# First chunk of a selective-scan layer: channel input projected without its convolution taps, convolution done on the projection by ScalarE and the Vector engine

## What is computed

```python
u, res = jnp.split(x @ W_in, 2, axis=-1)                 # 256 -> 2 x 512 channels
up = jnp.pad(u, ((0, 0), (2, 0), (0, 0)))
u = up[:, :L] * W_conv[:, 0] + up[:, 1:L + 1] * W_conv[:, 1] + up[:, 2:L + 2] * W_conv[:, 2]
u = jax.nn.silu(u)
x_dbl = u @ W_x
dt, Bm, Cm = jnp.split(x_dbl, [DT_RANK, DT_RANK + D_STATE], axis=-1)
delta = jax.nn.softplus(dt @ W_dt + b_dt)
# deltaA = exp(delta * A), deltaB_u = delta * u * B; scan h = deltaA * h + deltaB_u; y = h . C
# y = (y + u * D_param) * silu(res);  y @ W_out;  x + that, layer norm, experts
```

## Time and profile before

| what | us |
|---|---|
| median of 3 runs | 2549.71 |
| lowest and highest run | 2549.22 and 2555.29 |
| span of the profiled execution | 2526.0 |
| first scan of chunk 0 starts, from the span's start | 51.59 |
| PE, DVE, ACT, POOL busy, share of the span | 91%, 87%, 68%, 72% |
| mean granted TensorE clock | 0.970 |

### The profile page before, as it was taken

The page is one execution under the profiler, slowest core; times in us unless marked ns, Lnnn a source line. Parts: engine busy times, 40 slices in busy tenths (PEclk is TensorE's granted clock), DMA queues, the critical chain, the costliest instruction groups (busy, mean ns, idle before and its releaser), DMA issues. The chain is left out here.

```text
span 2526.0 us, 40011 instructions
## 1 busy us (share of the span) xinstructions
PE 2299.8 (91%) x14043; PEld 1789.0 (71%) x14043; DVE 2208.6 (87%) x2980; ACT 1726.0 (68%) x2861; POOL 1808.3 (72%) x859
## 2 busy tenths in 40 slices
PE   8999999999999999999999998643999999999995
PEld 3566666766766766666667666532989989989995
DVE  3899999999999999999999999987687677777775
ACT  3788888888888898888888888733344344334345
POOL 1698998988988989889899899724155445435566
PEclk9999999999999999999999999975999999999998
DMA  2211222222222221122122121112032322322353
GB/s 91 68 54 65 76 67 76 59 68 68 76 68 68 67 76 60 67 78 75 60 76 76 59 68 59 59 67 71 22 72 37 84 67 36 87 65 37 87 172 149
DMA packets 88227, 179.10 MB, mean 71 GB/s; under 512 B 8896, under 2 KB 51136, under 8 KB 88016
## 3 DMA queue, kind: packets, MB, share of 16 engines
q1 hardware_dynamic: 73136, 154.11, 18.5%
q0 software_dynamic: 14880, 22.29, 4.7%
HBM read 140.19 MB, written 36.18 MB: 70 GB/s over the span
## 5 line engine op out<-in xcount | busy, mean ns | idle before, releaser
L444 POOL TENSOR_TENSOR dbu<-du,b_all 128x2048 f32<-128x2048 f32 x255 | 1157.6, 4548 | 154.3 <-DVE hst L710 104.9
L533 ACT ACTIVATE da<-delta,a_neg 128x512 f32<-128x512 f32 x1008 | 689.5, 689 | 158.7 <-DVE hst L710 149.1
L710 DVE TENSOR_TENSOR_SCAN hst<-da,carry,dbu 128x512 f32<-128x512 f32 x504 | 618.0, 1266 | 0.7
L710 DVE TENSOR_TENSOR_SCAN hst<-da,dbu 128x512 f32<-128x512 f32 x504 | 589.0, 1206 | 18.2 <-ACT da L533 14.9
L1944 PE MATMUL gu<-x_part,w_part 128*128 128x384 f32 (+1 forms) x2304 | 492.0, 363 | 5.8 <-POOL w_part L1481 4.1
L1944 PEld LDWEIGHTS gu<-x_part,w_part 128*128 128x128 f32 x2304 | 407.7, 191 | 37.9 <-issue 4.4
L847 PEld LDWEIGHTS hd<-ident,hst 128*128 128x128 f32 x2048 | 236.0, 142 | 249.5 <-issue 118.9
L640 DVE SCALAR_TENSOR_TENSOR yacc<-hd,c_tok,yacc 128x512 f32<-128x512 f32 x512 | 371.8, 726 | 20.0 <-PE hd L847 19.4
L847 PE MATMUL hd<-ident,hst 128*128 128x128 f32 x2048 | 319.4, 279 | 75.5 <-DVE yacc L640 75.2
L789 PE MATMUL gen<-xT,w_u 128*128 128x512 f32 x720 | 359.7, 599 | 3.9 <-issue 2.7
L520 ACT ACTIVATE hTC<-w,c_tok 128x512 f32<-128x512 f32 x512 | 345.2, 674 | 20.6 <-PE w L847 20.6
(11 more groups left out here) (277 smaller groups left out, 2813.5 us busy)
## 6 DMA issues: line engine op xcount, KB each, us to landing
b_all<-b_rows SPq DMA_DIRECT2D x128, 512.0 KB, 3.8
xT<-in_xT SPq DMA_DIRECT2D x16, 514.0 KB, 5.2
xT_r<-in_xT SPq DMA_DIRECT2D x16, 512.0 KB, 5.1
x_rows<-in_x SPq DMA_DIRECT2D x16, 512.0 KB, 4.8
x_dram<-x SPq DMA_DIRECT2D x16, 512.0 KB, 3.0
acc_dram<-x SPq DMA_DIRECT2D x16, 512.0 KB, 4.5
w_raw<-in_wg SPq DMA_DIRECT2D x8, 1024.0 KB, 5.1
w_raw<-in_wu SPq DMA_DIRECT2D x8, 1024.0 KB, 8.0
```

The source lines that it names most:

```text
L444: nc.gpsimd.tensor_tensor(dbu[DBU[n]][:], du[parity][:], b_n, ALU.mult).then_inc(dbu_ready, 1)
L533: nc.scalar.activation(da_bank[t % 2][:], delta[parity][:, t, :], ACT.Exp, scale=a_neg[:, t, n:n + 1]).then_inc(da_ready, 1)
L710: nc.vector.tensor_tensor_scan(hst[DBU[n]][:, t, :], decay[:], dbu[DBU[n]][:, t, :], initial, ALU.mult, ALU.add).then_inc(scanned, 1)
```

## The change

For chunk 0 alone TensorE multiplies the input with the plain `W_in` (8 matmuls in place of 24), as it lies in `w_staging`, and only the input position of the last tap. ScalarE then copies each bank to `u_raw` with the last tap as a scale for each partition, and the Vector engine adds the two other taps with one `scalar_tensor_tensor` each, from the same bank shifted by one and two columns. Silu then reads `u_raw`. The copy of tile t + 1 stands before the Silu of tile t in ScalarE's order. The taps come in a further small weight tile `w_conv` (128 partitions by 12 values), with a DMA of its own. The load of `xT` moves ahead of the broadcast of the taps. `w_u` is made as before, for the chunks after; TensorE waits for it at the end of its lead.

```diff
+        w_conv = sb("w_conv", [P, DT, N_TAPS])
...
             sp.dma_start(w_staging, w_in_d[:, :, 0:DI]).then_inc(w_loaded, 16)
+            sp.dma_start(xT[:], xT_d[:, :, 0:CL + 2]).then_inc(xt_loaded, 16)
+            sp.dma_start(w_conv[:], a["W_conv"]).then_inc(conv_loaded, 16)
             sp.dma_start(gate[:, 0:N_TAPS, :], a["W_convT"].rearrange("(o t) d -> o t d", o=1).to_broadcast(
                 [P, N_TAPS, DI])).then_inc(spread_loaded, 16)
-            sp.dma_start(xT[:], xT_d[:, :, 0:CL + 2]).then_inc(xt_loaded, 16)
...
         def _(act):
-            for t in range(DT):
-                act.wait_ge(ring_full, LEAD.index(f"e{t}") + 1)
-                nc.scalar.activation(u[:, t, :], lead_bank[f"e{t}"][:], ACT.Silu).then_inc(lead_u if t < DT - 1 else u_ready, 1)
+            act.wait_ge(conv_loaded, 16)
+            for t in range(DT + 1):
+                if t < DT:
+                    act.wait_ge(ring_full, LEAD.index(f"e{t}") + 1)
+                    nc.scalar.activation(u_raw[:, t, :], lead_bank[f"e{t}"][:], ACT.Copy,
+                                         scale=w_conv[:, t, N_TAPS - 1:N_TAPS]).then_inc(lead_scaled, 1)
+                if t > 0:
+                    act.wait_ge(lead_conv, t)
+                    nc.scalar.activation(u[:, t - 1, :], u_raw[:, t - 1, :], ACT.Silu
+                                         ).then_inc(lead_u if t < DT else u_ready, 1)
...
+            dve.wait_ge(conv_loaded, 16)
+            for t in range(DT):
+                dve.wait_ge(lead_scaled, t + 1)
+                for back in range(1, N_TAPS):
+                    if back > 1:
+                        dve.wait_ge(lead_tap, t + 1)
+                    nc.vector.scalar_tensor_tensor(
+                        out=u_raw[:, t, back:], in0=lead_bank[f"e{t}"][:, 0:CL - back],
+                        scalar=w_conv[:, t, N_TAPS - 1 - back:N_TAPS - back], in1=u_raw[:, t, back:],
+                        op0=ALU.mult, op1=ALU.add).then_inc(lead_tap if back == 1 else lead_conv, 1)
...
         def _(pe):
             pe.wait_ge(xt_loaded, 16)
-            for tap in range(N_TAPS):
-                pe.wait_ge(taps_ready, tap + 1)
-                for t in range(DT):
-                    for k in range(KD):
-                        last = nc.tensor.matmul(lead_bank[f"e{t}"][:], w_u[:, tap, k, t * P:(t + 1) * P],
-                                                xT[:, k, tap:tap + CL], start=tap == 0 and k == 0,
-                                                stop=tap == N_TAPS - 1 and k == KD - 1)
-                    if tap == N_TAPS - 1:
-                        last.then_inc(ring_full, 1)
+            pe.wait_ge(w_loaded, 16)
+            for t in range(DT):
+                for k in range(KD):
+                    last = nc.tensor.matmul(lead_bank[f"e{t}"][:], w_staging[:, k, t * P:(t + 1) * P],
+                                            xT[:, k, N_TAPS - 1:N_TAPS - 1 + CL], start=k == 0, stop=k == KD - 1)
+                last.then_inc(ring_full, 1)
...
             pe.wait_ge(late_in, N_LATE * 16)
+            pe.wait_ge(taps_ready, N_TAPS)
```

More of the change, by code:

```diff
@@ L232, in attention @@
         spread_loaded = sem("spread_loaded")
+        conv_loaded = sem("conv_loaded")
+        lead_scaled = sem("lead_scaled")
+        lead_tap = sem("lead_tap")
+        lead_conv = sem("lead_conv")
         weights_in = sem("weights_in")
@@ L2033 @@
         "x": g["x"], "xT": padded.reshape(BATCH * (SEQ + 2), DM).T, "W_in": g["W_in"],
-        "W_convT": g["W_conv"].T, "W_x": g["W_x"],
+        "W_conv": g["W_conv"].reshape(DT, P, N_TAPS).transpose(1, 0, 2), "W_convT": g["W_conv"].T, "W_x": g["W_x"],
         "W_dt": g["W_dt"], "b_dt": g["b_dt"].reshape(DT, P).T, "D_param": g["D_param"].reshape(DT, P).T,
```

## The result

The changed kernel took 2538.81 us (median of 4 runs, 2537.26 to 2540.93) against 2551.53 for the kernel before (4 runs, 2549.22 to 2555.29): 12.7 us less. The ratio of the two medians is 0.995; the estimate from all runs is 0.994, with a 95% interval of 0.9929 to 0.9952, which is 12 to 18 us. Timed again in a later series, it took 2510.56 against 2524.74: 14.2 us less, ratio 0.9945 (0.9932 to 0.9959). The forecast was 2537.7 (2533 to 2543).

What follows compares the result with a forecast made beforehand. The Vector engine, 97% busy, was taken to bound the chunk stages, behind a lead of one chain to the first scan at 51.59 us. Saving 12.0 there gave 2549.7 - 12.0 = 2537.7 us, range 2533 to 2543.

Steps and rivals of the forecast that it cites:

- the 23.7 us added to the span: Whole kernel: the run median stood 23.7 us above the profile's span, so this was added to the forecast span of 2514.0.
- What carries over: After the lead: whatever is saved before the first scan shifts all that follows by as much; 12.0 us forecast.
- a sign of being wrong: After the lead: the first scan comes earlier but the distance from there to the end, forecast 2474.4 us, grows.
- Step 1: Loads in the lead: xT, moved ahead, lands at 7.3 us; the taps' broadcast at 9.6, plus 0.1 for w_conv.
- Step 2: TensorE's projection in the lead: 9.7 us from 7.35 in place of 23.4, with the last tile's bank full at 17.05.
- Step 3: Vector engine in the lead: free at 14.0, then eight added instructions of 0.75 us each, 6.0 in all, to 20.0.
- Step 4: ScalarE in the lead: copies and Silus keep ahead of the Vector engine; a possible second table load costs 0.1 us.
- e0: TensorE's projection in the lead: the PSUM bank of tile 0, first to fill and be copied; forecast full at 11.0 us.
- Step 5: End of xd in the lead: only two records remain after the last Silu; xdT copied at 21.8, not 36.65, saving 14.85.
- Step 6: TensorE's clock in the lead: pauses make it fall around xd's end, so 12.0 us is saved, not 14.85.
- rival (a): TensorE's clock in the lead: stays up through the d matmuls, so 14.85 us saved, 2534.9; chance 0.27.
- Rivals (b) to (d): Respectively: no change within 0.3%, 0.08; slower as w_conv shifts SBUF tiles, 2557, 0.03; tiles ready no earlier, 2549.7, 0.02.

Runs made afterwards that it cites:

- series 4: Kernels timed together on a chip numbered 4: four further variants of the changed kernel; the kernel before took 2558.50 us there.
- series 2: Kernels timed together on a chip numbered 8: both kernels again unedited, and two load-order variants; changed 2510.56 us against 2524.74, ratio 0.9945.

## Why the prediction was right

The time and its sign were right, and so was the mechanism: the lead is one chain, it gets shorter, and all that follows moves with it. The forecast for the first scan was 39.6; it came at 37.22, so 14.4 us saved and not 12.0. That the time came out within 1.1 us of the forecast is in part luck. By the medians 12.7 us were saved, by the trace 14.4, and the interval of the ratio covers both. And the 23.7 us added to the span were mostly the long rest of the timed runs; they came out because the runs of the changed kernel in that series had the long rest as well. Step by step:

- **What carries over.** Predicted 1:1. From the first scan to the experts' second load it is 1690.2 to 1692.9 us in all 14 profiles, for first scans between 34 and 53. Shown, within 2.7 us. The distance to the end, which the prediction put at 2474.4, was 2498.3 in the first profile and 2471.9 in the second. The first of these is what the prediction had named as a sign of being wrong; it was the profile that showed it and not the change, since kernels that don't differ there show the same in series 4 and not in series 2. What makes it stays open.
- **Step 1.** xT landed at 7.55 (predicted 7.3), the broadcast at 10.16 (9.7). Both late by 0.3 to 0.5. That w_conv costs 0.1 was right for its place; in another it cost 1.7 to 2.4, by one profile.
- **Step 2.** The projection took 10.1 us (9.7), e3 was full at 17.65 (17.05).
- **Step 3.** The Vector engine began its row at 14.35 (14.0), ended it at 20.46 (20.0); 0.74 to 0.75 each, as taken from L640 in the earlier trace rows.
- **Step 4.** The second table load ran where it was foreseen, 14.96 to 16.24, and cost little: Silu 0 waited for it, copy 2 came late, and the vector row stood still for 0.17 us. The 2.66 us for a switch of the Trainium skill ("ScalarE: Activation LUTs", "What ACT_TABLE_LOAD costs") didn't appear: the next activation started 1.29 us after the start of the load. What I had not foreseen is a load that waits. The first one stood behind the wait for e0 and ran at 11.41, where that of L452 had run at 1.95; it stayed hidden, since the Vector engine wasn't free before 14.35. Why the one waits and the other doesn't is not shown.
- **Step 5.** xdT at 22.28 (21.8): the sum of the small delays above.
- **Step 6, the step that failed.** "I take 12.0: a fall around xd's end." The clock stayed up to 27.2, and rival (a), with 0.27, described what happened: 14.85 by its sum, 14.4 measured. I had reasoned that xd with gaps is thin work, and had read the Trainium skill's warning of idle gaps as one of gaps like these, though it describes longer ones; the gaps were to be 0.65 us and were 0.25 and 0.38. The doubled vector work, with pauses of 1.6 to 1.7 us, shows that the mechanism exists. Its price ahead of the exponential was 2.7 us (2.8 by the prediction), and 0.9 for the last part of xd (0.95). The sum lacks a further 0.9 us: the copy of cT, which comes late and holds up the additions.
- **Rivals (b) to (d).** The table was not reloaded at every change between Copy and Silu: one load. Scans take 1211 ns (median) where they took 1208, and the stages take 1691.3 us in both, so w_conv's 48 bytes don't matter to them. The lead did what it says: the row of eight began at 14.35, not at 27.

## What to carry to other kernels

A chain ahead of the main loop, with nothing beside it, is worth its full length, and idle engines there take work almost for nothing: 16 matmuls (13.3 us) were exchanged for eight vector instructions (6.1 us) and four copies, and leaving the eight out again gave only 0.6 to 1.0 us. Before moving such work, write down the second bound (here the order of TensorE's own queue), since removing the first alone gives only the distance between them. When a new load is put in a queue, look at what lands behind it: 6 KB in the wrong place went with a landing 1.7 to 2.4 us later.

## What the runs showed that I had not expected

- Four one-input instructions on the Vector engine, 0.87 us in all, took 5.89 beside GpSimd's three; eight with a PSUM input were not slowed.
- A load of 6 KB between two large ones moved what landed behind it by 1.7 to 2.4 us (one profile), and at another place in the queue by nothing.
- TensorE's clock stayed up through xd with pauses of 0.25 to 0.45 us between its parts, and fell ahead of the last part with pauses of 1.6 to 1.7. Behind xd it fell in every kernel, 3.1 to 5.8 us after the copy of xd where it was still up then, and an early fall reached the first scan through cT, whose copy stands ahead of the additions.
- The experts' part took 779 to 783 us in some series and 807 to 817 in others, for the same instructions, with waits on ScalarE for which the trace names no releaser on the core. Only kernels timed in the same series can be compared here.
